# The router's logits as row sums on VectorE, with weight rows streamed by GpSimd, in a fused attention and mixture-of-experts kernel

## The reference

```python
x = x + tanh(g_xattn[0]) * xattn(layernorm(x), ctx, mask)      # q, k, v, softmax, out projection
y = layernorm(x)
gate_weights = softmax(y @ gate_w + gate_b)                    # gate_w is [512, 8]
topk_vals, topk_idx = top_k(gate_weights, 2)
h = gelu(y @ w1[n] + b1[n]); h = gelu(h @ w2[n] + b2[n])       # for the chosen experts n
x = x + tanh(g_ffn[0]) * sum(topk_vals * (h @ w3[n] + b3[n]))
```

## Time and profile before

| | us |
|---|---|
| median of 3 runs | 1781.81 |
| the profiled execution | 1782.03 |
| its span | 1780.0 |
| TensorE busy (PE) | 1763.5 |
| VectorE busy (DVE) | 1168.4 |
| ScalarE busy (ACT) | 961.1 |
| GpSimd busy (POOL) | 113.9 |

### The profile page before, as it was taken

How to read it: one execution, slowest core, us unless ns; L and a number is a source line. 1 busy time by engine, 2 the same in 40 slices (tenths; PEclk the granted TensorE clock), 3 DMA queues, 4 the chain that set the end, 5 groups by cost and what they waited for, 6 DMA issues and landing times.

```text
span 1780.0 us, 39543 instructions
## 1 busy us (share of the span) xinstructions
PE 1763.5 (99%) x14862; PEld 1534.2 (86%) x14862; DVE 1168.4 (66%) x3158; ACT 961.1 (54%) x1794; POOL 113.9 (6%) x159
## 2 busy tenths in 40 slices
PE   9999999999999999999999999999999999999997
PEld 8888888888888888888888877877899999999996
DVE  5666666667666666666666456566677777777772
ACT  4655656565555556565555535445555555545551
POOL 1100000000000000000000010000000110010010
PEclk9999999999999999999999999999999999999998
DMA  8981111111111111111103389998666666666661
GB/s 266 354 306 38 48 49 60 38 48 49 36 47 54 54 38 48 48 56 42 43 11 118 131 311 393 356 353 305 213 207 209 207 209 214 218 218 218 218 195 36
DMA packets 114268, 269.73 MB, mean 152 GB/s; under 512 B 15283, under 2 KB 33715, under 8 KB 114128
## 3 DMA queue, kind: packets, MB, share of 16 engines
q1 hardware_dynamic: 99664, 225.46, 36.9%
q0 software_dynamic: 14464, 42.35, 8.1%
HBM read 221.10 MB, written 46.66 MB: 150 GB/s over the span
## 4 chain that ended last, share of the span: by engine, by line
PE 96%; DMA 2%; DVE 1%; ACT 1%; issue 0%; POOL 0%; DVEq 0%; SPq 0%; ACTq 0%; POOLq 0%
PE bank_rows L2307 21%; PE bank_rows L690 16%; PE bank_rows L676 15%; PE bank_rows L738 8%; PE bank_rows L2322 7%; PE bank_rows L728 5%; PE bank_rows L749 4%; PE bank_rows L2361 4%; PE bank_rows L2388 3%; PE bank_rows L2347 3%; PE bank_rows L713 3%; PE bank_rows L765 3%; PE bank_rows L828 2%; DMA stage<-in_L_ffn_w 1%; PE bank_rows L752 1%; PE bank_rows L814 1%
## 5 line engine op out<-in xcount | busy, mean ns | idle before, releaser
L1142 ACT ACTIVATE probs<-probs,neg_max 100x722 f32<-100x722 f32 x248 | 220.9, 891 | 101.9 <-DVE neg_max L1494 101.9
L1487 DVE CUSTOM_DVE_ANT_0 probs<-bank_rows,mask_sb 100x362 f32<-100x362 f32 x496 | 234.6, 529 | 11.0 <-PE bank_rows L728 6.8
L2551 DVE TENSOR_TENSOR w_low<-stage,w_high 128x1024 fp32r<-128x1024 f32 x176 | 212.9, 1223 | 33.8 <-ACT w_high L2455 33.5
L1147 ACT ACTIVATE p_t<-bank_rows 121x600 f32<-121x600 f32 x256 | 171.7, 671 | 76.0 <-PE bank_rows L738 72.4
L2478 ACT ACTIVATE gelu<-bank_rows,biases 128x256 f32<-128x256 f32 x176 | 82.2, 473 | 222.3 <-PE bank_rows L2307 193.2
L2455 ACT ACTIVATE w_high<-stage 128x1024 fp32r<-128x1024 f32 x176 | 183.4, 1056 | 32.9 <-DMA stage<-in_L_ffn_w 31.6
L2307 PE MATMUL bank_rows<-h_low,w_high 128*128 128x256 f32 x704 | 199.2, 283 | 0.0
L2307 PE MATMUL bank_rows<-h_high,w_low 128*128 128x256 f32 x704 | 199.2, 283 | 0.0
L2307 PE MATMUL bank_rows<-h_high,w_high 128*128 128x256 f32 x704 | 199.2, 283 | 0.0
L676 PE MATMUL bank_rows<-ctx_high,wk_high 128*128 128x360 f32 (+1 forms) x512 | 182.7, 357 | 0.8 <-DVE ctx_low L1453 0.7
L738 PE MATMUL bank_rows<-ident,probs 100*121 100x100 f32 x1488 | 180.6, 257 | 1.3 <-ACT p_t L1147 1.3
(11 more groups left out here) (246 smaller groups left out, 3720.9 us busy)
## 6 DMA issues: line engine op xcount, KB each, us to landing
stage<-in_L_ffn_w SPq DMA_DIRECT2D x240, 512.0 KB, 4.3
plain_w<-in_L_ffn_w SPq DMA_DIRECT2D x15, 2048.0 KB, 12.1
expert_in_rows<-filling POOLq DMA_DIRECT2D x8, 3341.0 KB, 15.0
ctx_raw<-in_ctx SPq DMA_DIRECT2D x16, 720.0 KB, 4.9
ctx_raw<-in_ctx SPq DMA_DIRECT2D x15, 724.0 KB, 4.3
xs_sb<-expert_in_rows SPq DMA_DIRECT2D x11, 514.0 KB, 5.8
b_sb<-in_L_ffn_b SPq DMA_DIRECT2D x19, 256.0 KB
mask_sb<-in_mask_BxSxS_ff SPq DMA_DIRECT2D x16, 282.0 KB
```

The source lines that it names most:

```text
L1142: nc.scalar.activation(p, p, ACT.Exp, bias=neg_max[:, h:h + 1], scale=-1.0, accum_out=exp_sum[:, h:h + 1]).then_inc(probs_ready, 1)
L1147: nc.scalar.activation(p_t[:, h % HQ, :, :].rearrange("t (k i) s -> t k (i s)", k=2), bank_rows[0:TT, 4:6, 0:3 * S], ACT.Copy).then_inc(pt ...
L1487: nc.vector.tensor_tensor_reduce(out=probs_of(b, g)[:, q, at], in0=score_bank[q][0:S, 0:size], in1=mask_sb[:, at], scale=-1.0, scalar=BIG, ...
L2551: nc.vector.tensor_tensor(lo, src, hi.bitcast(F32), ALU.subtract).then_inc(chunk_lo[which], 1)
```

## The change

In bodies 1 to 14 (batches 0 to 13) the units X2T and LG go. The logits are made on VectorE by eight instructions for each batch (`dots`, `tensor_tensor_reduce` as in `score`): each multiplies `x2` [100 x 512] with one expert's weights, repeated over the 100 rows, and sums along the row into one column of `logits`. Each waits for the one before it, for `x2`, and for its weights. The weights come from a new input `gw_rows` [8 x 512], one DMA of 200 KB for each expert and batch, issued by GpSimd into four slots `router_rows`; a slot is loaded again when its dot is done, so the load for expert e + 4 is issued after dot e. Slot 3 lies over `filling` and is first loaded when all region fills have landed. `biased` adds the bias.

The order around it moves too. On TensorE XT stands where it fills the place of X2T, one step later, behind the first half of group 2's scores. `norm_in` and `ln_apply` for batch b + 2 move forward on VectorE to the end of group 1, `rstd_start` on ScalarE to behind head 6's exp, and the copy of XT to before K20's. The dots stand in five places: 0 and 1 before a `keys_low` of group 1's stretch, 2 after the first scored half of group 2, 3 and 4 after `scale_o` of group 1, 5 to 7 after V1. `choose` moves behind the next `keys_low`, `route_exps` behind the copy of head 9, and `carry` behind `scale_o` of group 2. Batches 14 and 15 keep X2T and LG; there `place` comes before `carry`.

```diff
@@ -197,13 +197,13 @@
 TAIL = ("A3", "Y", "X2T", "LG", "CNT")
 AFTER_LAST = ("Y", "A3", "X2T", "LG", "CNT")
 EVEN_BODY = ("K31", "A3", "V3", "Y", "V4",
-             "V5", "V0", "A0", "K00", "K10", "X2T",
-             "K20", "LG", "A1", "V1", "K01", "K11",
-             "XT", "K30", "CNT", "A2", "Q01", "V2", "K21")
+             "V5", "V0", "A0", "K00", "K10",
+             "XT", "K20", "A1", "V1", "K01", "K11",
+             "K30", "CNT", "A2", "Q01", "V2", "K21")
 ODD_BODY = ("K31", "A3", "V3", "Y", "V4",
-            "V5", "V0", "A0", "Q23", "K00", "X2T",
-            "K20", "LG", "A1", "V1", "K10", "K01",
-            "XT", "K30", "CNT", "A2", "V2", "K11", "K21")
+            "V5", "V0", "A0", "Q23", "K00",
+            "XT", "K20", "A1", "V1", "K10", "K01",
+            "K30", "CNT", "A2", "V2", "K11", "K21")
 FIRST_BODY = ("K31", "V3", "V4", "V5",
               "V0", "A0", "V1", "K00", "XS",
               "K10", "A1", "V2", "K20", "K01",
...
@@ -211,10 +211,13 @@
 LAST_QUERIES = tuple("Q" if u == "Q01" else u for u in EVEN_BODY if u != "XT")
 LAST_BODY = ("K31", "A3", "V3", "Y", "V4", "V5",
              "A0", "A1", "X2T", "A2", "LG", "CNT")
+
+IN_ROWS = B - 2
+ROUTER_SLOTS = 4
 LAST_TURNS = LAST_BODY.index("A0")
 PRO = -1
 RUN_UP = 15
-SAME_BANK = {("LG", "A1"), ("CNT", "A2"), ("XT", "A2")}
+SAME_BANK = {("CNT", "A2"), ("XT", "A2")}
 
 
 ALL_UNITS = {}
...
@@ -332,6 +335,10 @@
     scatter_go = sem("scatter_go")
     rows_scattered = sem("rows_scattered")
     table_step = sem("table_step")
+    router_loaded = [sem(f"router_slot_{k}_loaded") for k in range(ROUTER_SLOTS)]
+    router_dot = sem("router_dot")
+    biased_step = sem("biased_step")
+    router_go = sem("router_go")
     early_step = sem("early_step")
 
     place = Places(nc, shared_from)
...
@@ -446,6 +455,9 @@
     early_first = place("early_first", [1, 1])
     blocks_of = place("blocks_of", [1, 2, E + 1])
 
+
+    router_rows = [place(f"router_rows_{k}", [S, D]) for k in range(ROUTER_SLOTS - 1)]
+    router_rows.append(nc.alloc_sbuf_tensor_at("router_rows_last", [S, D], F32, offset=filling_at))
     assert shared_from + place.at <= nc.sbuf_top, place.at
 
 
...
@@ -516,11 +528,21 @@
                                 base=0, pattern=[[1, E], [-1, E]], channel_multiplier=0).then_inc(route_consts, 1)
         assert made + 1 == ROUTE_CONSTS
 
+        def load_router(e):
+            k = e % ROUTER_SLOTS
+            pool.dma_start(router_rows[k][:], gw_rows[e:e + 1, :].broadcast_to([S, D])
+                           ).then_inc(router_loaded[k], 16)
+
         for e in range(E):
             pool.wait_ge(scored, 6 * e + 1)
+            if e == E - 1:
+                for k in range(ROUTER_SLOTS - 1):
+                    load_router(k)
             pool.dma_start(xs_dram[e * REGION:(e + 1) * REGION, :].rearrange("(t p) d -> p t d", p=P),
                            filling[:, 0:1, :].broadcast_to([P, REGION // P, ROW])).then_inc(regions_filled, 16)
         pool.wait_ge(regions_filled, 16 * E)
+        pool.wait_ge(spare_filled, 32 * TPB)
+        load_router(ROUTER_SLOTS - 1)
 
         def scatter(b):
 
...
@@ -532,7 +554,18 @@
                     out=xs_dram, out_offset=bass.IndirectOffsetOnAxis(ap=pair_row[:, k:k + 1], axis=0),
                     in_=x2[:, k, :], in_offset=None).then_inc(rows_scattered, 16)
 
-        with pool.Fori(0, B) as b:
+        def pass_router(b, upto):
+
+            for e in range(upto):
+                pool.wait_ge(router_dot, E * b + e + 1)
+                pool.sem_inc(router_go, 1)
+                load_router((e + ROUTER_SLOTS) % E)
+
+        with pool.Fori(0, IN_ROWS - 1) as b:
+            pass_router(b, E)
+            scatter(b)
+        pass_router(IN_ROWS - 1, E - ROUTER_SLOTS)
+        with pool.Fori(IN_ROWS - 1, B) as b:
             scatter(b)
         pool.wait_ge(rows_scattered, 32 * B)
 
...
@@ -928,11 +961,11 @@
                 transpose_probs(b, 6)
                 keys(b, n, 1, 0, BACK)
             transpose_probs(b, 7)
-            transpose_x2(b, t)
 
             scores(b, 2, 0)
+            if b + 2 < B:
+                transpose_xn(b, b + 2)
             keys(b, n, 2, 0)
-            router_logits(b, t)
             scores(b, 2, 1)
             attend(b, b, odd, 1)
             values(b, 1)
...
@@ -944,8 +977,6 @@
             transpose_probs(b, 10)
             keys(b, n, m, 1, BACK)
             transpose_probs(b, 11)
-            if b + 2 < B:
-                transpose_xn(b, b + 2)
 
             scores(b, 3, 0)
             keys(b, n, 3, 0)
...
@@ -1249,6 +1280,8 @@
             exps(b, 5)
             copy_probs(b, 4)
             exps(b, 6)
+            if b + 2 < B:
+                rstd_start(0, b + 2)
             if odd:
                 copy_probs(b, 5)
                 exps(b, 7)
...
@@ -1262,27 +1295,24 @@
                 copy_probs(b, 6)
                 keys_high(b, n, 1, 0)
             copy_probs(b, 7)
-            copy_transposed(b, "X2T", x2t[:])
+            second_copy(t)
+
             if b + 2 < B:
-                rstd_start(0, b + 2)
-            second_copy(t)
-
+                copy_transposed(b, "XT", xt[:, :, slot(b + 2), :])
             keys_high(b, n, 2, 0)
             recip_copy(b, 1)
             exps(b, 8)
             exps(b, 9)
             copy_probs(b, 8)
-            route_exps(t)
             exps(b, 10)
             keys_high(b, n, *((1, 0) if odd else (0, 1)))
             copy_probs(b, 9)
+            route_exps(t)
             exps(b, 11)
             copy_probs(b, 10)
             keys_high(b, n, 0 if odd else 1, 1)
             copy_probs(b, 11)
 
-            if b + 2 < B:
-                copy_transposed(b, "XT", xt[:, :, slot(b + 2), :])
             keys_high(b, n, 3, 0)
             recip_copy(b, 2)
             exps(b, 12)
...
@@ -1540,6 +1570,27 @@
             if k in HELD_AFTER:
                 held()
 
+        def dots(t, es):
+
+            for e in es:
+                k = e % ROUTER_SLOTS
+                dve.wait_ge(x2_ready, t + 1)
+                if E * t + e > 0:
+                    dve.wait_ge(router_dot, E * t + e)
+                dve.wait_ge(router_loaded[k], 16 * (E // ROUTER_SLOTS * t + e // ROUTER_SLOTS + 1))
+                nc.vector.tensor_tensor_reduce(
+                    out=dot_rows[:], in0=x2[:, 0, 0:D], in1=router_rows[k][:], scale=1.0, scalar=0.0,
+                    op0=ALU.mult, op1=ALU.add, accum_out=logits[:, e:e + 1]).then_inc(router_dot, 1)
+
+        def biased(t):
+            dve.wait_ge(router_dot, E * (t + 1))
+            nc.vector.tensor_tensor(logits[:], logits[:], gb_sb[:], ALU.add).then_inc(biased_step, 1)
+            dve.wait_ge(biased_step, t + 1)
+
+        def less_max(t):
+            route_then(t, 1, nc.vector.reduce_max(row_max[:], logits[:], AX.X))
+            route_then(t, 2, nc.vector.tensor_scalar(shifted[:], logits[:], row_max[:, 0:1], None, ALU.subtract))
+
         def logits_out(body, t):
             bank, done = take(body, "LG")
             nc.vector.tensor_tensor(logits[:], bank[0:S, 0:E], gb_sb[:], ALU.add).then_inc(done, 1)
...
@@ -1571,10 +1621,9 @@
             route_then(t, k + 4, nc.vector.tensor_scalar(token[:], token[:], float(S), None, ALU.add))
 
         def place(body, t):
-            k = STEP_EITHER
             bank, done = take(body, "CNT")
             _, fills = unit(body, "CNT")
-            route_then(t, k + 5, nc.vector.tensor_tensor(row_of[:], bank[0:S, EARLIER:EARLIER + E],
+            route_then(t, STEP_EITHER + 1, nc.vector.tensor_tensor(row_of[:], bank[0:S, EARLIER:EARLIER + E],
                                                          next_row[0:S, :], ALU.add))
             nc.vector.tensor_tensor(next_row[:], bank[:, IN_ALL:IN_ALL + E], next_row[:], ALU.add).then_inc(done, 1)
             dve.wait_ge(done, fills)
...
@@ -1762,33 +1811,35 @@
             norm_out(t)
             score(b, 1, 1)
             values_out(b, 1 - odd, 0)
+            if b + 2 < B:
+                norm_in(b + 2)
             scale_o(b, b, 0)
             ctx_low(n, 2)
             ctx_low(n, 3)
+            if b + 2 < B:
+                ln_apply(0, b + 2, x_ln[:], xn[:], xn_ready)
             if odd:
                 queries_low(b, "Q23")
-                if b + 2 < B:
-                    norm_in(b + 2)
+                dots(t, (0, 1))
                 keys_low(b, n, 0, 0)
             else:
                 keys_low(b, n, 0, 0)
-                if b + 2 < B:
-                    norm_in(b + 2)
+                dots(t, (0, 1))
                 keys_low(b, n, 1, 0)
             recips(b, 1)
 
             score(b, 2, 0)
-            logits_out(b, t)
+            dots(t, (2,))
             keys_low(b, n, 2, 0)
             score(b, 2, 1)
             scale_o(b, b, 1)
-            logits_less_max(b, t)
+            dots(t, (3, 4))
             values_out(b, 1 - odd, 1)
-            if b + 2 < B:
-                ln_apply(0, b + 2, x_ln[:], xn[:], xn_ready)
```

(25 more changed lines are left out.)

1 line of the change is left out of this document (removed).

## The result

The changed kernel takes 1790.49 us, median of 6 runs (1788.41 to 1792.46), against 1782.24 for the kernel before (6 runs on the same chip): a ratio of 1.0045, 95% interval 1.0034 to 1.0055. It is slower by 0.45%. The prediction said 1783, range 1771 to 1797, and gave "slower" 0.30: the range holds, the likeliest case does not. The profiled execution took 1788.41, its span is 1786.6.

What follows compares the result with a forecast made beforehand. TensorE, busy for 99% of the span, was taken as the bound. 1782.0 less 0.4 us over 14 batches plus 2.0 once for the first changed batch gave 1783.6, 1783.4 against the median, said as 1783; range 1771 to 1797.

Steps and rivals of the forecast that it cites:

- forecast A: The wait for slot 3 gives back nearly all of TensorE's gain; 1780 to 1787 us, no change, chance 0.36.
- rival C: Slot 3's load takes longer, T = 4.6; each batch loses 0.57 us; 1792 us, slower, chance 0.24.
- TensorE's saving: X2T gone saves 0.39 us and LG gone 0.55: 0.94 us per batch, 13.2 over 14, the ceiling.
- The move of the norm's steps: ScalarE's two small norm steps, ahead of head 5's copy, cost TensorE 0.3 us in even batches, nothing in odd ones.
- The dots: Eight VectorE dots of 512 columns: main part 0.61 to 0.75 us, 0.73 taken per dot, 5.8 us a batch.
- rival D: VectorE dots run at half rate, 1.26 us each; 35 us lost, 1818 us, slower, chance 0.06.
- T: Time from dot 3's end until dot 7's rows have landed in slot 3: 4.0 us, bounds 3.8 and 5.3.
- The chain from there to group 3's scores: Dot 7, bias, `shifted`, ScalarE's exps and copy, head 11's transposes, scores: forecast 3.82 us in the even batch.
- break-even: The T at which a batch neither gains nor loses: 3.96 us in the even batch, 4.1 in the odd.
- The contention: Dot 4's two SBUF inputs may contend with GpSimd issuing slot 3's load; T could grow by up to a dot.
- The first batch: Slot 3 over `filling` waits for all region fills, ready near 133.5, wanted at 131.5: once 2 us, bounds 0 and 3.
- The cover of dots 5 to 7: These VectorE dots, unlike dots 0 to 4, have no idle time to hide in and delay `shifted`.

Runs made afterwards that it cites:

- five-slot kernel with the early start: Changed kernel with a fifth weight slot, and first-batch loads for dots 4 to 6 issued before GpSimd's wait for the region fills: 1770.39 us, ratio 0.9937.
- the room alone (four slots, early order): Changed kernel, slot 3 still over `filling`, first-batch loads for dots 4 to 6 issued before GpSimd's wait for the region fills: 1785.73 us, ratio 1.0023.
- The narrow dots: Five-slot kernel with the early start, each dot cut from 512 columns to 16: 1770.25 us against 1770.39.
- the exps behind the copy: Changed kernel with ScalarE's `route_exps` moved behind head 11's exp and the copy of head 10's probs: 1789.52 us, ratio 1.004.
- the quarter loads: Changed kernel with its reloads cut to 128 of 512 columns, 50 KB instead of 200 KB: 1779.86 us, ratio 0.9989.
- the later slot: Changed kernel with dot 7's rows in slot 0, so their load is issued after dot 4 instead of dot 3: 1820.01 us, ratio 1.0205.

## Why the prediction went as it did

The mechanism is that of forecast A; the time, 1790.49, lies above A's 1780 to 1787 and below rival C's 1792.

**TensorE's saving (0.94 a batch, 13.2): right.** The five-slot kernel with the early start shows 13.0 in the busy line and -0.9 a batch in the offsets.

**The move of the norm's steps (0.3 lost in an even batch): wrong.** The offset falls by 0.58 up to the second scores of group 2, not by 0.25. With no such charge it would fall by 0.53 (0.94 less 0.41), so none is to be seen. It made the even batch no better, because a lead of TensorE ahead of the hole is worth little: the hole ends with the load, and only what reaches dot 3 moves that. Dot 3 came 0.11 earlier than forecast against the batch's start (564.26 less 4.41, against 559.96).

**The dots: right in size.** 0.69 against 0.61 to 0.75, 0.82 from one dot's start to the next where the next was waiting, 0.73 to the bias. I took 0.73 everywhere: 0.1 short between dots, which the wait before dot 7 swallows. No half rate, so rival D is out: the instruction reads two float32 tensors from SBUF and an accumulator (688 ns for 512 columns, 529 with one input in PSUM for 361: 1.34 and 1.47 ns a column). The half rate that the Trainium skill's Vector Engine (DVE) Microarchitecture Reference, "Points that are easy to get wrong", gives for one form with two such inputs isn't seen here; whether this instruction has that form, no run shows.

**T: the right term, a little short.** From the end of dot 3's read (564.95) to the load's issue are 0.59 us (0.5 taken), from there until dot 7 runs 3.51 (3.5 taken): 4.10 against 4.0. The odd batch has 4.05. In the profiles of the three runs that keep the four slots' turn, the loads' size and ScalarE's order, T is 3.90, 3.92 and 3.98 on average, against 4.10 here. The chain from there to group 3's scores takes 0.15 more than worked out (569.05 to 573.02 is 3.97, forecast 3.82; most of it between the start of ScalarE's copy and the transposes, 0.79 instead of 0.70, and from those to the scores, 0.69 instead of 0.65). For the even batch shown: 4.10 - 3.96 + 0.15 - 0.11 = +0.18, and the offsets say 4.59 - 4.41 = +0.18. For the odd batch behind it, where dot 3 comes 0.14 later than forecast: 4.05 - 4.10 + 0.16 + 0.14 = +0.25, and the offsets say 4.85 - 4.60. The mean of 13 batches is the same 0.18. So this is case A, with T moved by 0.1 and the chain by 0.15 towards C. A term that sits on its break-even can't be called by its sign: 0.2 us in 8 decide it, 14 times over.

**The contention** that the Trainium skill's SBUF — State Buffer, "Who interferes with whom", would allow isn't needed to explain a T of 4.10; no run separates it.

**The first batch (2 us): mis-sized, with half of the reason.** It cost 3.7. Most of the miss is the clock, for which the step had no term: 1.5 of the 3.7. The 2.15 before it agree with the forecast's 2, but partly by luck. The step named only slot 3's room, and dot 3 itself waited for 1.0 us, not 2; it missed that GpSimd's program is a queue too: the loads for dots 4 to 6 stood behind the wait for the fills, with which they have nothing to do. With the room alone (four slots, early order) the offset before the clock's share is 1.66.

**The sum.** From the forecast's 1783.6 for the profiled execution: +1.7 for the first batch, 0.18 + 0.03 over 13 batches +2.7, and 0.6 behind the attention part give 1788.6, against 1788.41 measured. All of these misses lie on one side, and the range's width had room for them. One sum of the forecast is off, and nothing hangs on it: rival C at T = 5.3 comes to 1802, not 1800. The median of six runs lies 2.1 above that execution, at granted clocks of 0.995 to 0.997; whether the clock fell in further batches there wasn't recorded batch by batch, and stays open.

**The cover of dots 5 to 7.** The forecast feared none. The narrow dots show that 0.5 us less of each gains nothing once the load is in time, so the loss in the steady batches was one wait, not VectorE's 75 us of new work.

## What to carry to other kernels

Where a buffer is refilled after its use, count from the end of the last reader to the next reader, with wake, issue and landing in it (here 4.1 us for 200 KB, and 4.5 in the run where the load stood right behind another), and let the slots turn so that the tightest pair has that much between; one slot more was worth 0.8% here. An engine that issues DMAs is a queue: a load behind an unrelated wait is late even when its own buffer has been free for long. And a hole in TensorE may cost more than its length: 2.7 us became 4.2 in the first batch by the clock behind it.

## What the runs showed of the hardware

- The granted clock fell to half behind TensorE's hole in the first changed batch wherever that was 1.7 us or longer (1.71 with the exps behind the copy, 1.86 with the quarter loads, 2.40 to 4.06 in five others), and in the run with the later slot behind ten holes of 1.84 to 3.12 us, the first batch's among them; there it stayed up behind three of 2.07, 2.15 and 2.39 us. Behind holes of up to 1.5 us it never fell in the changed part of these runs. In all of them, the kernel before too, it is at half for the last 6 to 10 us of the span. So the length of the hole alone doesn't decide; what else does is open.
- A broadcast load of 200 KB into slot 3 on GpSimd's queue lands in 3.4 us (median, 3.2 to 4.0), one of 50 KB in 2.8 (2.8 to 4.3), and about 0.6 us goes by in front of it, from the dot's end to the issue. A straight line through the two medians leaves some 2.6 us without bytes, an estimate.
- The landing's median varies by 0.2 us from one profiled run to another, and the steady batch with it: medians of 3.2 to 3.3 in the three other runs with full loads that keep the four slots' turn and the order on ScalarE, where the steady batch cost -0.03, -0.01 and +0.06 instead of +0.18. As they hold both rooms of slot 3, the room isn't the reason; what is stays open.
